# adaLN block on one Trainium2 core: variances and modulation steps interleaved on TensorE, squares between halves of a scaling, quarters of the next chunks moved

## The reference

```
mod = (silu(c) @ wmod).reshape(2, 6, 1, -1)         # wmod 1024 x 6144; sa, ca, ga, sb, cb, gb
ga, gb = signed, magnitude at least 0.25
h = layernorm(x) * (1 + ca) + sa
x = x + ga * attention(h)     # scores over the 2 batch entries, for each of 1024 features,
                              # summed over the 2048 tokens; adds its input
h = layernorm(x) * (1 + cb) + sb
x = x + gb * ((silu(h @ Wgate.T) * (h @ Wup.T)) @ Wdown.T)      # 2752 hidden features
```

## Time and profile before

| | us |
|---|---|
| median of 3 runs | 2857.48 (2857.2 to 2865.62) |
| the profiled execution's own time | 2861.89 |
| its span | 2860.1 |
| PE busy in it | 2756.5 (96%) |
| DVE, ACT, POOL busy | 1546.1, 1059.2, 157.8 |
| mean granted PE clock | 0.987 |

### The profile page before, as it was taken

The page is one execution under the profiler, slowest core; times in us unless marked ns, Lnnn a source line. Parts: engine busy times, 40 slices in busy tenths (PEclk is TensorE's granted clock), DMA queues, the critical chain, the costliest instruction groups (busy, mean ns, idle before and its releaser), DMA issues.

```text
span 2860.1 us, 32536 instructions
## 1 busy us (share of the span) xinstructions
PE 2756.5 (96%) x11784; PEld 2162.0 (76%) x11784; DVE 1546.1 (54%) x2057; ACT 1059.2 (37%) x1616; POOL 157.8 (6%) x206
## 2 busy tenths in 40 slices
PE   8986999999899999999999899999999999999999
PEld 3334777777788887788887788887788888888887
DVE  7796776775455443545453443334546545546444
ACT  4456455444333332333333211111433333343332
POOL 5300000001001101001100000000000000000000
PEclk9998999999999999999999999999999999999999
DMA  8574788988978888978888999999757667667654
GB/s 364 197 299 147 279 304 313 330 303 302 302 274 302 314 284 277 309 273 308 312 284 260 347 349 352 354 342 342 249 214 261 212 225 246 216 225 254 231 207 166
DMA packets 359711, 795.77 MB, mean 278 GB/s; under 512 B 25760, under 2 KB 154016, under 8 KB 350848
## 3 DMA queue, kind: packets, MB, share of 16 engines
q1 hardware_dynamic: 341648, 721.32, 72.0%
q0 software_dynamic: 17088, 59.78, 6.1%
q10 hardware_dynamic: 816, 12.58, 1.0%
HBM read 553.26 MB, written 240.32 MB: 277 GB/s over the span
## 4 chain that ended last, share of the span: by engine, by line
PE 87%; DMA 4%; DVE 3%; issue 2%; ACT 2%; SPq 1%; POOL 1%; DVEq 0%; ACTq 0%; POOLq 0%
PE ps L1583 18%; PE ps L1584 18%; PE ps L1585 18%; PE ps L1646 10%; PE ps L1647 10%; PE ps L1648 10%; PE ps L1456 2%; DMA h_dram<-ww 1%; DMA x_raw_P<-xr_dram 1%; PE ps L1483 1%; DMA xbuf<-x 1%; SPq L386 1%; PE ps L1541 0%; DMA wm<-wmod 0%; POOL sq_pair L570 0%
## 5 line engine op out<-in xcount | busy, mean ns | idle before, releaser
L1583 PE MATMUL ps<-x_hi_P,w_slot 128*128 128x512 f32 (+1 forms) x1848 | 725.1, 392 | 24.4 <-ACT vv L799 9.1
L1584 PE MATMUL ps<-x_lo_P,w_slot 128*128 128x512 f32 (+1 forms) x1848 | 723.6, 392 | 0.0
L1585 PE MATMUL ps<-x_hi_P,w_slot 128*128 128x512 f32 (+1 forms) x1848 | 723.1, 391 | 0.0
L1646 PE MATMUL ps<-hh,w_hi 128*128 128x512 f32 (+1 forms) x1232 | 481.1, 390 | 3.2 <-DVE w_lo L1350 1.9
L1647 PE MATMUL ps<-hl,w_hi 128*128 128x512 f32 (+1 forms) x1232 | 480.9, 390 | 0.0
L1648 PE MATMUL ps<-hh,w_lo 128*128 128x512 f32 (+1 forms) x1232 | 479.9, 389 | 0.0
L1583 PEld LDWEIGHTS ps<-x_hi_P,w_slot 128*128 128x128 f32 (+1 forms) x1848 | 344.5, 186 | 106.0 <-ACT vv L799 10.4
L1585 PEld LDWEIGHTS ps<-x_hi_P,w_slot 128*128 128x128 f32 (+1 forms) x1848 | 344.8, 187 | 78.8
L1584 PEld LDWEIGHTS ps<-x_lo_P,w_slot 128*128 128x128 f32 (+1 forms) x1848 | 344.8, 187 | 77.2
L1350 DVE TENSOR_TENSOR w_lo<-w_raw,w_hi 128x1408 fp32r<-128x1408 f32 x112 | 181.8, 1623 | 213.0 <-ACT w_hi L866 213.0
L1583 PE MATMUL ps<-x_hi_P,w_hi 128*128 128x512 f32 (+1 forms) x616 | 245.8, 399 | 45.6 <-issue 20.0
(11 more groups left out here) (181 smaller groups left out, 2599.4 us busy)
## 6 DMA issues: line engine op xcount, KB each, us to landing
w_slot<-whl_dram SPq DMA_DIRECT2D x420, 512.0 KB, 6.1
w_raw<-wds_dram SPq DMA_DIRECT2D x64, 704.0 KB, 4.7
hl_raw<-h_dram SPq DMA_DIRECT2D x56, 768.0 KB, 7.0
h_dram<-hb SPq DMA_DIRECT2D x30, 1280.0 KB, 9.6
whl_dram<-w_hi SPq DMA_DIRECT2D x140, 256.0 KB, 3.6
whl_dram<-w_lo_P SPq DMA_DIRECT2D x140, 256.0 KB, 4.1
w_raw<-wdn SPq DMA_DIRECT2D x48, 704.0 KB, 4.8
hl_raw<-h_dram SPq DMA_DIRECT2D x28, 1024.0 KB, 9.8
```

Of the source, the lines that this page charges most:

```text
L1583: mm(bank, hi[:, w], x_hi[name][:, k, :], start=fresh and k == 0, stop=False, skip_group_check=not fresh)
L1584: mm(bank, hi[:, w], x_lo[name][:, k, :], start=False, stop=False, skip_group_check=not fresh)
L1585: ins = mm(bank, lo[:, w], x_hi[name][:, k, :], start=False, stop=k == KH - 1, skip_group_check=not fresh)
L1646: mm(bank, hi[0:n, w], hh[stage % 2][0:n, j, :], start=fresh and j == 0, stop=False, skip_group_check=not fresh)
```

## The change

In the statistics, each step of a variance is followed by a quarter of a modulation part (two k of eight), where whole parts stood between pairs of variances. In t = 1 the variances come directly after the means, before any part. For the first pair, ACT squares the first half of the differences of h = 0 after the first four slices of `scaled_f(1)`; `root_f(1)` moves ahead of `modulate_f(0)`; PE takes `variance_f(1)` before the four late parts. The last wmod part gets a tile of its own (`wm_late[3]`, over memory that `u_f[0]` used) and is loaded between the two x2 stores. ACT's wait for `mod_done` 23 becomes one for 22, behind `modulate_f(0, KH..)`. P7's operand is subtracted before P5's lo half, P6's at product 2 and P4's at 3. For s = 0 the quarters start at products 9, 37, 65, 93 (before 4, 34, 64, 94).

```diff
-    return M_S * s + (4 + 30 * r if s == 0 else 6 + 29 * r)
+    return M_S * s + (9 + 28 * r if s == 0 else 6 + 29 * r)
...
             for h in range(2):
                 sp.wait_ge(x2f_ready, KD * (h + 1))
                 sp.dma_start(x2_first[h], x_f[:, h].rearrange("p k b c -> p (k b c)")).then_inc(x2f_stored, 16)
-            load_part(NPART - 1)
+                if h == 0:
+                    sp.dma_start(wm_late[3][:], wmod[NPART - 1]).then_inc(wm_last_loaded, 16)
...
-            scaled_f(1)
+            scaled_f(1, range(KH))
+            squares_f(0, range(2))
+            scaled_f(1, range(KH, KD))
             s.activation(eps_root, eps_t, ACT.Sqrt)
-            squares_f(0)
+            squares_f(0, range(2, NSQ))
             root_f(0)
             w_hi_cast(0)
             w_hi_cast(1)
-            squares_f(1)
+            squares_f(1, range(NSQ))
+            root_f(1)
             act.wait_ge(xh_stored[0], 32)
             for k in range(KH):
                 modulate_f(0, k)
-            root_f(1)
             act.wait_ge(rawf_ready, KH)
             s.copy(x_hi["P1"][:], raw_b11[:]).then_inc(xhi_ready, 1)
-            act.wait_ge(mod_done, NPART - 1)
             for k in range(KH, KD):
                 modulate_f(0, k)
             act.wait_ge(x2f_stored, 32)
             act.wait_ge(rawf_ready, KD)
+            act.wait_ge(mod_done, FIRST[3] + 2)
...
             for m in range(4, EARLY):
                 w_hi_cast(m)
+            for k in range(KH, KD):
+                modulate_f(1, k)
             x_hi_first("P5")
-            for k in range(KH, KD):
-                modulate_f(1, k)
...
             w_lo_part(4)
+            dve.wait_ge(rawf_ready, 2 * KD)
+            v.tensor_tensor(x_raw["P7"][:], x_raw["P3"][:], x_raw["P6"][:], ALU.subtract).then_inc(sumsf_ready, 1)
             x_lo_part(0, "P5")
...
             def variances(u, h, group=None, part_of=None):
...
                         mm(ps_var[h], ones[:], sq_pair[:, j % 2, :], start=j == 0, stop=j == NSQ - 1).then_inc(sq_pair_used, 1)
+                        if group is not None:
+                            modulate(group, part_of, range(2 * j, 2 * j + 2))
...
                     parts(0, range(2))
-                    variances(1, 0)
-                    variances(1, 1)
-                    parts(0, range(2, 4))
+                    variances(1, 0, 0, 2)
+                    variances(1, 1, 0, 3)
                 else:
...
-                    parts(0, range(4, GROUP[0]))
-                    parts(1, range(2))
-                    variances(0, 0)
-                    variances(0, 1)
-                    parts(1, range(2, 4))
-                    variances(1, 0)
-                    variances(1, 1)
-                    parts(1, range(4, GROUP[1]))
+                    variances(0, 0, 0, 4)
+                    variances(0, 1, 0, 5)
+                    variances(1, 0, 1, 0)
+                    variances(1, 1, 1, 1)
+                    parts(1, range(2, GROUP[1]))
...
-            parts(3, range(2))
             variance_f(1)
-            parts(3, range(2, GROUP[3]))
+            parts(3, range(GROUP[3]))
```

More of the change, by code:

```diff
@@ L130, in build @@
     wm = [sb(f"wm{r}", [KD, WPART], F32, (148 + 8 * r) * K) for r in range(WM_RING)]
-    wm_late = [sb(f"wm_late{r}", [KD, WPART], F32, a * K) for r, a in enumerate((96, 104, 126))]
+    wm_late = [sb(f"wm_late{r}", [KD, WPART], F32, a * K) for r, a in enumerate((96, 104, 126, 32))]
     sq = sb("sq", [2, SQ_PER, T], F32, 172 * K)
@@ L250, in build @@
     wm_loaded = [sem(f"wm_loaded{r}") for r in range(WM_RING)]
+    wm_last_loaded = sem("wm_last_loaded")
     silu_zeroed, silu_ready, mod_done = sem("silu_zeroed"), sem("silu_ready"), sem("mod_done")
@@ L338, in load_part @@
                     sp.wait_ge(xh_stored[0], 32)
-                to = wm if w < FIRST[3] else wm_late
-                sp.dma_start(to[w % WM_RING][:], wmod[w]).then_inc(wm_loaded[w % WM_RING], 16)
+                to = wm[w % WM_RING] if w < FIRST[3] else wm_late[w - FIRST[3]]
+                sp.dma_start(to[:], wmod[w]).then_inc(wm_loaded[w % WM_RING], 16)
             def load_pair(a):
@@ L693, in _, with scaled_f @@
             act.wait_ge(coef_ready, 1)
-            def scaled_f(h):
-                for k in range(KD):
+            def scaled_f(h, ks):
+                for k in ks:
                     for n in range(NB):
@@ L705, in root_f, with squares_f @@
                 s.activation(std_f[:, h, :], ps_var_f[h], ACT.Sqrt, bias=eps_t, scale=1.0 / D).then_inc(stdf_ready, 1)
-            def squares_f(h):
-                for j in range(NSQ):
+            def squares_f(h, js):
+                for j in js:
                     n = NSQ * h + j
@@ L737, in modulate_f @@
                 ins.then_inc(rawf_ready, 1)
-            scaled_f(0)
+            scaled_f(0, range(KD))
             copy_rows(2)
-            scaled_f(1)
+            scaled_f(1, range(KH))
+            squares_f(0, range(2))
+            scaled_f(1, range(KH, KD))
             s.activation(eps_root, eps_t, ACT.Sqrt)
-            squares_f(0)
+            squares_f(0, range(2, NSQ))
             root_f(0)
@@ L1182, in x_first @@
                 if i == 2:
-                    dve.wait_ge(rawf_ready, 2 * KD)
-                    v.tensor_tensor(x_raw["P7"][:], x_raw["P3"][:], x_raw["P6"][:], ALU.subtract).then_inc(sumsf_ready, 1)
-                if i == 3:
                     dve.wait_ge(sumsf_ready, 2)
                     v.tensor_tensor(x_raw["P6"][:], x_raw["P7"][:], raw_b11[:], ALU.add).then_inc(sumsf_ready, 1)
+                if i == 3:
                     dve.wait_ge(sumsf_ready, 3)
@@ L1447, in _, with modulate @@
             pe.wait_ge(ones_ready, 1)
-            def modulate(weights, bank, j, group):
+            def modulate(group, j, ks):
+                w, bank = FIRST[group] + j, ps_rows[group]
+                weights = wm[w % WM_RING] if w < FIRST[3] else wm_late[w - FIRST[3]]
+                if ks[0] == 0:
+                    if w == NPART - 1:
+                        pe.wait_ge(wm_last_loaded, 16)
+                    else:
+                        pe.wait_ge(wm_loaded[w % WM_RING], 16 * (w // WM_RING) + 16)
                 rows, block, cols = ROWS[group], j // 2, slice(j % 2 * WPART, (j % 2 + 1) * WPART)
                 start = max(ROWS) - NB - block * NB
-                for k in range(KD):
+                for k in ks:
                     ins = mm(bank[0:rows, cols], silu_pad[:, k, start:start + rows], weights[:, k, :],
                              start=j == k == 0, stop=j == GROUP[group] - 1 and k == KD - 1)
-                ins.then_inc(mod_done, 1)
+                if ks[-1] == KD - 1:
+                    ins.then_inc(mod_done, 1)
             def turn(group, bank, rows, at):
@@ L1470, in parts @@
                 for j in js:
-                    w = FIRST[group] + j
-                    pe.wait_ge(wm_loaded[w % WM_RING], 16 * (w // WM_RING) + 16)
-                    modulate((wm if w < FIRST[3] else wm_late)[w % WM_RING], ps_rows[group], j, group)
+                    modulate(group, j, range(KD))
             for t in range(NPAIR // 2):
@@ L1487, in means, with variances @@
                     ins.then_inc(mean_mm, 1)
-                def variances(u, h):
+                def variances(u, h, group=None, part_of=None):
                     i = 2 * u + h
```

## The result

The changed kernel takes 2822.29 us, the median of four runs (2818.56 to 2823.07). The kernel before took 2858.11 beside it (2857.2 to 2865.62). The ratio is 0.9866, with a 95% interval of 0.9847 to 0.9885: 35.8 us less. The forecast was 2815.0 in a range of 2800 to 2838.

What follows compares the result with a forecast made beforehand. PE, busy 96% of the span, was taken as the bound, leaving its idle time and slow stretches. Terms 7.4 + 5.4 + 3.7 + 17.0 + 8 + 1 = 42.5 took 2861.89 to 2819.4, 2815.0 against the median; range 2800 to 2838.

Steps and rivals of the forecast that it cites:

- the coefficients' term: Statistics of t = 0 and t = 1: coefficients at 161.5 instead of 169.40, -7.9 us, bounds -12.7 and -4.
- Rival B: Statistics give little: coefficients only 4 us sooner, -8 for -12.8 at first product, DMA takes back quarters' 8; 2827; chance 0.23.
- C: Rival that everything opens: part 15 not late (-4.8 more), all 18.56 us in the quarters gained (-10); 2801; chance 0.13.
- First pair: Coefficients to P6: -7.4 us up to mean_f(1), then -5.4 to the first product (224.3), then -3.7 at P6.
- First quarter: From P6 to the end of product 14: DVE finds quarter-0 loads landed or waits up to 2 us; -17.0 us.
- the form of D with late loads: First quarter's POOL loads land late because DVE is working; first loads then give 13 us; this form given little.
- D: Rival: new wait at o = 21 or late loads at product 13; quarters cost 4 us; 2831 to 2840; chance 0.12.
- F: Rival that the kernel gets slower through ACT's wait at o = 21, 2875 at 20 us beyond its lead; chance 0.03.
- Overlapped quarters: Stretch 300 to 620: less of the 18.56 us in which PE isn't busy; -8 us, bounds +4 and -17.
- The clock: PE's idle pieces in 300 to 620: some 2 us each by the skill's rule, nothing by the rows; sum took nothing.
- Transition: Last quarter ends one product earlier, before the transition to the next pair: -1 us, bounds 0 and -2.7.

Runs made afterwards that it cites:

- e10: Changed kernel with the variances of t = 0 put back in front of their whole parts, as before: 2818.22 us, ratio 0.9862.
- e4: Changed kernel with the first half's x-hat store of t = 1 issued later, behind all sums of squares: 2817.58 us, ratio 0.9858.
- e8: Changed kernel with the t = 1 store late, part 19 in quarters inside variance_f(0), group 2's copy_rows and turn moved behind it: 2813.98 us, ratio 0.9847.
- e11: Changed kernel with scaled_f(1) whole ahead of squares_f(0), the squares undivided: 2820.19 us, ratio 0.9867.
- e6: Changed kernel with two late parts again ahead of variance_f(1) and root_f(1) behind four modulations: 2822.73 us, ratio 0.9877.
- e9: Changed kernel with the quarters' old first start and new distance (4 + 28 r): 2829.07 us, ratio 0.9898.
- e3: Changed kernel with the quarters' new first start and old distance (9 + 30 r): 2843.58 us, ratio 0.9952.
- e5: The changed kernel, unaltered, timed a second time: 2821.08 us (2814.64 to 2824.02), ratio 0.9869.
- e12: e8 with t = 0 as before, part 19 whole between mean_f(0) and variance_f(0), and two weight casts behind root_f(1): 2814.66 us, ratio 0.9852.
- e7: Changed kernel with each variance of t = 1 done whole and its part whole behind it: 2822.5 us, ratio 0.988.

## Why the prediction was right, and where it was not

The direction, the places and most of the sizes held. The measured 2822.29 lies 7.3 above the forecast of 2815.0, just outside the forecast's own range (2807 to 2822) and inside the whole one. That the sum of the terms is nearer than this, -40.3 for -42.5, is in part luck: the coefficients' term fell 6.4 short, and the quarters and the transition gave 4.8 more than forecast.

- **Statistics: the step that failed.** Forecast -7.9 at the coefficients, measured -1.45 (169.40 to 167.95); the lower bound given was -4. Several sizes in it were off. A variance step with its quarter of a part was priced at 0.86 + 0.87 = 1.73 from runs of like matmuls; alternating, it takes 2.015. PE's means of t = 1 start at 62.57, 0.5 sooner than before, where I took 3.5. DVE leaves t = 0 at 86.47, 4.0 later than before (82.49), where I took 1.7. So the first normalisation came at 112.88 (forecast 111.8), four slow ones lay beside POOL's adds where I kept two, the store went out at 137.1 (133.9), and the chain of DVE was through at 153.0 (149.8).
- **The same step: which load is late.** DVE's lateness alone decided nothing (e10). What decided is which part is late: the wait for wmod is 5.91 us, and I had said 5.9, but it was for part 14 and not 15. That can be worked out from PE's share of these sizes, though no run tests it by itself. Part 14 can be loaded when part 11 is done. By my figures that is at 130.9 (117 and four parts of 3.47), 3.0 ahead of the store at 133.9; measured it was at 137.46, 0.33 behind the store. The steps of 2.015 make 4.6 us of PE's lateness, their later start 2.4. A load issued 2.3 to 3.1 ahead of the store still landed after 4.8 to 5.2, before and after. With the wait two parts, slow, stand between it and the turns instead of one: 8.92 in place of 5.5, and it ends later besides (150.25 against 147.2). Turns over at 161.0, forecast 154.6. That the wait and what follows hold the coefficients is shown by e4: without it the turns end at 152.8 and the coefficients come at 159.69.
- **What the forecast took for granted.** It let the gain at the coefficients go on to mean_f(0) whole. In the changed kernel that held: mean_f(0) ends 14.1 us after the coefficients (182.02 and 167.95), forecast 14.2. e4 shows on what it rests: there the coefficients are 8.3 sooner and mean_f(0) is at the same place, since PE's parts of group 2 stand ahead of it and the store, moved, makes one of their loads late. I had written that parts 16 to 19 end ahead of the need, which holds only as long as no load is late among them. e8, which removes that too, has the end of mean_f(0) 9.7 sooner than the changed kernel. Rival B's -8 at the first product is nearer to the measured -6.7 than my -12.8. Its reason (the transfers collide worse than once) is not what happened: PE waited once, one part too early. Its time of 2827 is too late because the quarters' 8 were not taken back. C fell at its first half: the part is late.
- **First pair.** From the coefficients to the end of mean_f(1) 34.6 us, forecast 36.1, before 35.65. The divided squares gave 0.6 of this (e11), where I had said nothing or a cost of 0.5. From there to the first product 27.8, before 32.0, forecast 26.7: -4.2 for -5.4. The wait of 10.96 went to 2.56 and comes back as 10.97 with e6. P6 is 20.95 behind the first product, forecast 20.9: -3.7 as said, though P6 still waits 3.15.
- **First quarter.** From P6 to the copy in group 1 the change is -16.9, forecast -17.0 to the end of product 14, where it is -16.9 too. DVE found its loads landed. They took 9.7 us with DVE at work, 9.9 before: the form of D with late loads didn't show. In the prediction I read the Trainium skill, "SBUF — State Buffer", section "Who interferes with whom", as if any work of DVE would hold such loads back. The section names copy, cast and tensor_scalar, and says that tensor_tensor was not seen to do it. DVE's work beside these loads was tensor_tensor but for four instructions of 0.2 us, so they don't test that rule. The normalisations beside POOL's adds (1.67 to 1.80 against 0.68) are where a wait between DVE and POOL does show.
- **Overlapped quarters.** G1 to G10 took 368.65 and takes 358.89: -9.8, forecast -8. e9 and e3 show that the distance makes it, not the start. The wait at o = 21 that I feared in D and F did appear, on ACT, 2.5 us in three pieces and the longest 1.5; PE never waits for it. My reason for only half of the 18.56 was a DMA share that would rise to 0.955; it rose to 0.93, and of PE's waits only the four at the sums over features are left, 7.0 us.
- **The clock.** Two stretches with one such wait each (460 to 480 above, 540 to 560 alike) have 0.91 and 0.92, where before 560 to 580, with 3.4 us of idle in pieces, had 1.00. The forecast took nothing for it. Of the four waits at the sums, those of 1.92, 2.29 and 2.30 us had the lower level of the clock behind them, that of 0.54 didn't. Before, a wait of 2.18 at the same matmuls had full clock behind it. The lines are after (the wait of 2.30 ended at 474.33), then before (the wait ended at 542.50):

```profile
476.00:478.00 2.00, 2.00 (x6) 1.52 (x6) 2.00 (x5) 0.63 (x1) 0.00 (x0) 0.50 0.70 262
```

```profile
542.00:544.00 2.00, 1.50 (x8) 1.32 (x9) 2.00 (x5) 0.96 (x2) 0.00 (x0) 1.00 1.04 377
```

By the Trainium skill, "TensorE: Matmul & The Clock Gate", section "HAM oscillation — how this bites in real kernels", an engine that goes idle between groups starts again at half clock; three waits after agree with it, and the wait and the pieces of before don't.
- **Transition and rest.** To group 11 -4.0, forecast -1; behind it +0.8. That is where the sum came back: -1.45 - 1.0 - 4.2 - 3.7 - 16.9 - 9.8 - 4.0 + 0.8 = -40.3, against -42.5. The runs' median moved by 35.8: the profiled execution before lay 3.8 above the median of its four runs, and that of after 0.7 below its own.

**What stays open.** A gain in front of the first product isn't passed on at a fixed rate: e6 loses 5.1 us there and 0.3 at G10, e8 gains 4.3 there and 7.8 at G10. That other waits of the first pass take up a delay is likely, but no run separates it. Nor is it known why 9 with 30 loses more than 4 with 30. e4 and e10 lie 4 to 5 us below the changed kernel's first series and 3 to 3.5 below e5; since e5 alone ran from 2814.64 to 2824.02, no cause is claimed for that.

**The best version** is e8, 2813.98 us, 0.9847 of before. e12 at 2814.66 can't be told from it.

## What to carry over

When a slow periodic chain is laid over a periodic loop on in-order engines, its distance and its first start are two choices: try the distance against the places where successive pieces meet on one engine (28 for 30 here; that it is a whole number of the loop's periods of 14 may be the reason, and wasn't tested), and put the first start behind its loads. When a wait is on the path, count what stands in the queue behind it before the next consumer, and ask of that consumer what else it needs: moving a store to remove a wait of 5.9 us gave 8.3 at the coefficients and nothing at the mean. When a small load may meet a big store, work out which of the two is asked for first. Interleave two kinds of matmul to hide a partner's pace, but price each switch from alternating rows and not from runs of like ones.

## What the runs showed of the hardware

- Switching between the two kinds of matmul costs time at full clock: 2.015 us for two 128x512 and four 128x256 in alternation, 0.86 + 0.87 in runs of their own. That is 0.14 us a switch. The changed kernel shows it sixteen times in a row with the same duration; what in the switch takes the time was not separated. Whole parts behind whole variances (e7) take 3.55 instead of 3.50, so only 0.05 is seen at that switch; at the switch back a wait for POOL hides it.
- A 1 MB load issued by SP beside a 4 MB store issued by ACT lands after 12.7 us (13.0 before); the four parts issued between 120 and 136 us, ahead of the store, land after 4.8 (median). When the store moves (e4), a load issued beside it lands after 13.0, and it is another part that PE waits for, 6.19 us.
- After one wait of 5.91 us, two parts take 8.92 us instead of 6.99: 1.9 us of slow clock come on top of the wait (0.63 granted in 150.25 to 155.30, 1.00 behind it).
